# Four engine programs written out for all 16 images in place of a loop, and the offset convolution moved one tile earlier on TensorE

## The chip, the cores and the metric

The kernel runs on one core of one Trainium2 chip. The metric is the device time of one execution in microseconds (us). Of the kernel before there are three such times, with a median of 4523.1 us (4519.83 to 4523.54), and one profiled execution.

## The reference

Sixteen images of 32 channels and 64 x 64 pixels go through four residual steps, each `x = x + f(norm(x))`. The norm subtracts the mean and divides by the standard deviation, for each image and channel.

1. A 3 x 3 convolution written in Winograd form with 6 x 6 tiles: a transform of the input, one product over channels for each of the 36 frequencies, and the inverse transform.
2. A deformable 3 x 3 convolution in 8 groups. A convolution with 18 outputs (the offset convolution) gives for each pixel and tap an offset in y and x; each tap is read by bilinear sampling at the shifted place and then weighted and summed.
3. Four quantised 3 x 3 convolutions one after the other, with weights that are plus or minus a scale, with rounding and clamping between them, and a 1 x 1 branch beside the second.
4. A 3 x 3 convolution plus a product over the absolute vertical differences, and a gate per channel from a small two-layer network on the channel means.

## The kernel before

Everything is in float32, except the three later quantised convolutions, which have bfloat16 operands. The 64 rows of an image are cut into 4 strips; strip and channel together fill 128 partitions, with 1024 pixels each.

The work of three images is interleaved. One period (n) holds 24 slots of 3 tiles, written (slot, tile), as (14, 2). In period n the kernel does the deformable sampling of image n, which is the bulk; step 1, the norm and the offset convolution of image n + 1 (the functions named `a`); steps 3 and 4 of image n - 1 (the functions named `c`); and the first norm of image n + 2 (`first`). The order on each engine is written out by hand in that engine's `slot`.

- TensorE has in each tile a row tile (`row_tile`, L1512, 6 products of 128 x 128 by 128 x 512, from `select` and `image` into `ps_r`), then at tile 0 the folds of the slot before (L1524, L1545), at some tiles the transposes of gathered samples (`turn`, L1538), and then what `a` and `c` have for that tile. `conv_half` (L1498) makes all 3 x 3 convolutions: the offset convolution from `taps_a` (shown as `wino`) into `ps_a`, and those of step 3 from `taps_c` into `ps_c`.
- VectorE multiplies each row tile by column weights (L1217), and works on the gathered samples, the norms and the rounding. It orders its own instructions by a counting semaphore (`Chain`).
- ScalarE makes `select` (L672, L674), copies the image that a period samples into `image` (`place_image`, L683: the first two thirds at the end of the period before, the last third at the head of the period), and takes results out of PSUM.
- SyncE issues transfers in order: the column weights (L481), the 12 shifted copies of the normalised image into `taps_a` (L434, at its slot 12), the store of the activations to a plane in memory (L439, at slots 6, 9 and 12) and the three loads of shifted planes into `taps_c` (L445, at slots 7, 10 and 13). `load_image` (L491, slot 22) brings the next image from the table of patches.
- GpSimd gathers the samples by indirect transfers, 192 for each image, in loops of its own.

`schedule` gives the order of the periods to the other four engines. Periods -2, -1, 0, 15 and 16 are written out; periods 1 to 14 are a hardware loop of 14 turns:

```python
    chain.restart()
    period(0)
    chain.restart()
    with eng.Fori(1, N - 1) as t:
        period(t)
        chain.restart()
    period(N - 1)
```

`restart` waits for the engine's own counting semaphore and clears it. In the loop, waits compare with values computed in registers from the period's number, and some addresses are computed too. The tiles that the change touches on TensorE are (14, 2), which has the third later convolution of step 3 (called conv3 below) and the offset convolution; (5, 2), which has the first convolution of step 3 (conv0) and two frequency products of step 1 (L1451).

Of the kernel before, what the change touches and what calls it, by code (L numbers as in the profile page):

```python
# [12 lines left out]
N, C, H, W = 16, 32, 64, 64  # L13
# [98 lines left out]
def live(n):  # L112
    return not isinstance(n, int) or 0 <= n < N
# [21 lines left out]
class Chain:  # L135
# [8 lines left out]
        return self.n  # L144

    def upto(self, n):
        self.eng.wait_ge(self.sem, n)

    def join(self):
        self.eng.wait_ge(self.sem, self.n)  # L150
# [2 lines left out]
        self.add(ins)  # L153
        self.join()

    def restart(self):
        if self.n:
            self.join()
            self.eng.sem_clear(self.sem)
            self.n = 0  # L160


def schedule(eng, chain, slot, prepare=None):

    def period(n):
        for s in range(SLOTS):
            slot(n, s)

    period(-2)
    period(-1)
    if prepare:
        prepare()
    chain.restart()
    period(0)
    chain.restart()
    with eng.Fori(1, N - 1) as t:
        period(t)
        chain.restart()  # L180
    period(N - 1)
    chain.restart()
    period(N)


def build(nc, x, w0, w1off, w1d, w2t, w2n, wds, w3t, w3e, watt1, watt2, vecs, off_bias, prelu_a, batt1, out):
    with ExitStack() as ctx:
# [175 lines left out]
        def tap_rows(t):  # L363
            return t.rearrange("p (r w) -> p r w", w=XW)
# [214 lines left out]
        @block.gpsimd  # L579
        def _(pool):  # L580
            chain = Chain(pool, pool_chain)
            for t in (values, xn_a, xn_c, act_c):
                nc.gpsimd.memset(t[:], 0.0).then_inc(zeroed, 1)
            pool.wait_ge(zeroed, 4)
            chain.step(nc.gpsimd.memset(same_channel[:], 0.0))
            nc.gpsimd.affine_select(out=ident[:], in_=zeros, compare_op=ALU.not_equal, fill=1.0, base=0,
                                    pattern=[[-1, P]], channel_multiplier=1).then_inc(idents_ready, 1)
            sc = same_channel[:].rearrange("p (s c) -> p s c", c=C)
            for s in range(STRIPS):
                chain.step(nc.gpsimd.affine_select(out=sc, in_=sc, compare_op=ALU.not_equal, fill=1.0 / STRIPS,  # L590
                                                   base=-s * C, pattern=[[0, STRIPS], [-1, C]], channel_multiplier=1))
            nc.gpsimd.memset(eps_col[:], EPS).then_inc(idents_ready, 1)
            pool.wait_ge(idents_ready, 2)

            for half in range(2):
                ps = slice(half * W, half * W + W)
                chain.step(nc.gpsimd.iota(grid_y[ps], pattern=[[2, Q], [1, 3]], base=half - 1,
                                          channel_multiplier=0, allow_small_or_imprecise_dtypes=True))
                chain.step(nc.gpsimd.iota(grid_x[ps], pattern=[[0, 3], [1, 3]], base=-1,
                                          channel_multiplier=1, allow_small_or_imprecise_dtypes=True))  # L600
            chain.step(nc.gpsimd.iota(minus_row[:], pattern=[[0, 1]], base=0, channel_multiplier=-1,
                                      allow_small_or_imprecise_dtypes=True))
            chain.step(nc.gpsimd.memset(one_col[:], 1.0))
            nc.gpsimd.memset(base_row[:], 0.0).then_inc(grid_ready, 1)
            pool.wait_ge(grid_ready, 1)
            chain.restart()
            pool.wait_ge(table_cleared, 16)
            freed = pool.alloc_register("freed")
            pool.reg_mov(freed, 1)
            with pool.Fori(0, N) as n:  # L610
                with pool.Fori(0, PARTS // IDX) as quad:

                    pool.wait_ge(table_out, (n + 1) * TABLE_OUT)
                    for h in range(IDX):
                        pool.wait_ge(idx_placed, n * PARTS + quad * IDX + (h + 1))
                        for j in range(JB):

                            pool.wait_ge(weighted, freed)
                            pool.reg_add(freed, freed, 1)
                            for k in range(GTAPS):  # L620
                                i = j * GTAPS + k
                                nc.gpsimd.indirect_dma_start(  # L622
                                    out=ring[j][:, h % 2, k, :], out_offset=None, in_=table,
                                    in_offset=bass.IndirectOffsetOnAxis(ap=idx_part[:, h, i:i + 1], axis=0),
                                ).then_inc(gathered[(h % 2) * JB + j], 16)
# [245 lines left out]
        def _(dve):  # L871
            v = nc.vector
            chain = Chain(dve, dve_chain)
# [371 lines left out]
            summed = [0]  # L1245

            def gathered_block(n, s, q):


                g, e = divmod(s, DT)  # L1250
                m, h = (n, g + 1) if g < PARTS - 1 else (n + 1, 0)
                if e == 0 and live(n):
                    if q == 0:
                        if s > 0:
                            chain.upto(summed[0])
                        add_columns(n, g, 1)
                        summed[0] = weigh_corners(n, g, 2)
                    if q == 1:
                        chain.upto(summed[0])
                        chain.upto(add_rows(g, 2))  # L1260
                        add_columns(n, g, 2)
                    if q == 2:
                        summed[0] = weigh_corners(n, g, 3)
                if e == 1 and live(n):
                    if q == 0:
                        chain.upto(summed[0])
                        summed[0] = add_rows(g, 3)
                    if q == 1:
                        chain.upto(summed[0])
                        add_columns(n, g, 3)  # L1270
                if e == 2 and live(m):
                    if q == 0:
                        if s == SLOTS - 1:
                            dve.wait_ge(a_dve.sem, a_dve.at(m, "weights"))
                        chain.upto(take_weights(h))
                        summed[0] = weigh_corners(m, h, 0)
                    if q == 1:
                        chain.upto(summed[0])
                        chain.upto(add_rows(h, 0))
                        add_columns(m, h, 0)  # L1280
                    if q == 2:
                        chain.upto(weigh_corners(m, h, 1))
                        summed[0] = add_rows(h, 1)
# [129 lines left out]
        def _(pe):  # L1413
# [28 lines left out]
            def a(n, s, q):  # L1442
                at = (s, q)
# [11 lines left out]
                    mean(a_dve, a_pe, n, "1", mv_a, ps_a)  # L1455
                if at == (11, 1):
                    var(a_dve, a_pe, n, "1", mv_a, ps_a)
                if at == (14, 2):
                    pe.wait_ge(a_dve.sem, a_dve.at(n, "norm1"))
                    pe.wait_ge(taps_a_in, n * COPIES_IN + COPIES_IN)  # L1460
                    for h in range(2):
                        conv_half(ps_a, h, w_off, 0, tap_rows(taps_a)).then_inc(a_pe.sem, 1)
# [66 lines left out]
            def turn(n, g, k):  # L1529
                part = n * PARTS + g  # L1530
                if k == 0:
                    pe.wait_ge(weighted, part * JB + (RING + JB))
                    if not known_zero(n) or g > 0:
                        pe.wait_ge(copied, part * CHUNKS)
                else:
                    pe.wait_ge(copied, part * CHUNKS + k)
                for j in range(JB):
                    ins = nc.tensor.transpose(ps_t[:, j * P:(j + 1) * P],  # L1538
                                              values[:, g % 2, j, chunk_start(k):chunk_start(k) + 4].rearrange("p k c -> p (k c)"), ident[:])
                ins.then_inc(turned, 1)  # L1540
# [62 lines left out]
            def slot(n, s):  # L1603
                g, e = divmod(s, DT)
                for q in range(WT):
                    if live(n):
                        row_tile(n, s, q)
                    if q == 0:
                        fold_before(n, s)
                    if live(n):  # L1610
                        if e == DT - 1 and q != 1:
                            if q == 0 and s in LAST_READ and live(n - 1):
                                pe.wait_ge(c_act.sem, c_act.at(n - 1, LAST_READ[s]))
                            turn(n, g, q // 2)
                    if live(n + 1):
                        a(n + 1, s, q)
                    if live(n - 1):
                        c(n - 1, s, q)
                    if live_s(n + 2):
                        first(n + 2, s, q)  # L1620

# [64 lines left out]
```

## Time and profile before

| | |
|---|---|
| median of three runs | 4523.1 us (4519.83 to 4523.54) |
| the profiled execution | 4541.68 us |
| its span, first to last instruction | 4539.9 us |
| mean granted TensorE clock | 0.970 of full |
| TensorE busy | 4235.0 us, 93% |
| VectorE, ScalarE, GpSimd busy | 65%, 41%, 68% |
| busy share of the DMA engines | mostly 0.7 to 0.8 |

The span is that of one execution under the hardware profiler. Matmuls overlap, so that a busy TensorE isn't one at its peak. Busy shares count an instruction's own time only; time in which an engine waits, branches or issues transfers is idle. "issue" as a releaser means that the engine waited for nothing that the profile shows.

### The profile page before, as it was taken

What the parts mean: (1) busy time and instruction counts of PE and PEld (TensorE: products, weight loads), DVE (VectorE), ACT (ScalarE), POOL (GpSimd) and SP (SyncE); (2) the same over time, 40 slices, a digit from 0 to 9 for tenths busy, and PEclk for the clock granted to TensorE, in tenths of its full rate; (3) what the DMA queues carried; (4) which work ended last, traced back from release to release, by engine and by line L of the source; (5) the groups of instructions that cost most, each with busy time, mean ns of one, the idle gap of its engine ahead of it and who ended that gap; (6) DMA issues with size and microseconds to landing.
All of it is one profiled execution on the core that took longest, in us unless ns stands there. A gap on an engine that the chain in (4) does not pass through costs nothing.

```text
span 4539.9 us, 75043 instructions
## 1 busy us (share of the span) xinstructions
PE 4235.0 (93%) x24997; PEld 2030.2 (45%) x24997; DVE 2948.8 (65%) x6076; ACT 1864.5 (41%) x2023; POOL 3088.7 (68%) x3094
## 2 busy tenths in 40 slices
PE   2899999999999999999999999999999999999993
PEld 2444444444444444444444444444444444444441
DVE  5656676666666766677666666766667666766553
ACT  1434444443434434444344434434444344444431
POOL 1777777676776767667677776767767677676750
PEclk8999999999999999999999999999999999999996
DMA  4687788778877787777778877787777777878862
GB/s 112 214 248 228 235 255 231 230 228 237 238 230 233 223 234 237 219 242 234 227 238 244 243 225 232 225 234 240 223 241 234 225 232 232 245 234 235 244 200 61
DMA packets 480356, 1024.07 MB, mean 226 GB/s; under 512 B 262165, under 2 KB 298357, under 8 KB 475637
## 3 DMA queue, kind: packets, MB, share of 16 engines
q1 hardware_dynamic: 324628, 511.64, 39.0%
q10 hardware_dynamic: 57024, 305.72, 20.0%
q0 software_dynamic: 98304, 201.52, 16.2%
q8 instruction: 233, 3.82, 0.3%
q14 instruction: 167, 1.36, 0.1%
HBM read 862.19 MB, written 73.20 MB: 206 GB/s over the span
## 4 chain that ended last, share of the span: by engine, by line
PE 70%; DMA 11%; SPq 7%; DVE 5%; issue 4%; POOL 2%; ACT 0%; ACTq 0%; DVEq 0%; another core or an unknown queue 0%; POOLq 0%
PE ps_r L1512 50%; PE ps_c L1498 6%; DMA taps_c<-plane_act 5%; PE ps_y L1524 5%; DMA plane_act<-act_c 3%; PE ps_a L1451 3%; SPq L434 3%; PE ps_c L1538 2%; POOL ring L622 2%; DMA wino<-patch_table 1%; PE ps_y L1545 1%; SPq L439 1%; PE ps_a L1489 1%; SPq L491 1%; DVE col_hat L1217 1%
## 5 line engine op out<-in xcount | busy, mean ns | idle before, releaser
L622 POOL DMA_INDIRECT ring<-patch_table,idx_part x3072 | 3080.5, 1003 | 1305.1 <-issue 1168.4
L1512 PE MATMUL ps_r<-select,image 128*128 128x512 f32 x6912 | 3183.7, 607 | 59.9 <-issue 48.3
L1512 PEld LDWEIGHTS ps_r<-select,image 128*128 128x128 f32 x6912 | 1270.3, 192 | 1481.8 <-issue 1459.2
L1217 DVE TENSOR_TENSOR col_hat<-ps_r,col_hat 128x512 f32<-128x512 f32 x1152 | 794.8, 690 | 1366.4 <-PE ps_r L1512 1359.0
L672 ACT ACTIVATE select<-row_in,minus_row 128x1536 f32<-128x1536 f32 x384 | 604.1, 1573 | 778.9 <-PE ps_r L1512 731.5
L674 ACT ACTIVATE select<-select,one_col 128x1536 f32<-128x1536 f32 x384 | 605.3, 1576 | 12.5
L691 ACT COPY samples<-ps_c 128x512 f32<-128x512 f32 x256 | 149.8, 585 | 679.1 <-PE ps_c L1538 679.1
L1524 PEld LDWEIGHTS ps_y<-col_hat,w_dense 128*32 128x32 f32 x9216 | 228.7, 109 | 297.1 <-issue 296.2
L1524 PE MATMUL ps_y<-col_hat,w_dense 128*32 128x128 f32 x9216 | 331.9, 277 | 0.0
L1226 DVE TENSOR_TENSOR ps_w<-ring,ps_w 128x384 f32<-128x384 f32 x512 | 284.7, 556 | 31.1 <-DMA ring<-patch_table,idx_part 21.5
L1232 DVE TENSOR_TENSOR ring<-ring,ps_w 128x384 f32<-128x384 f32 x512 | 280.2, 547 | 4.4
L1228 DVE TENSOR_TENSOR ring<-ring,ps_w 128x384 f32<-128x384 f32 x512 | 280.2, 547 | 0.0
L739 ACT ACTIVATE work_c<-ps_c,bn_bias,bn_scale 128x512 f32<-128x512 f32 x160 | 120.2, 778 | 216.8 <-PE ps_c L1498 202.9
L1242 DVE TENSOR_TENSOR values<-ring 128x192 f32<-128x192 f32 x512 | 182.5, 356 | 19.4
L1498 PE MATMUL ps_c<-taps_c,w_signs 96*32 96x512 bf16 x1152 | 92.7, 462 | 108.3 <-DMA taps_c<-plane_act 77.8
L707 ACT COPY wino<-ps_a 128x384 f32<-128x384 f32 x96 | 46.0, 479 | 310.6 <-PE ps_a L1451 310.6
L1538 PE MATMUL ps_c<-ident,values 128*128 128x128 f32 x1024 | 160.8, 280 | 0.0
L1538 PEld LDWEIGHTS ps_c<-ident,values 128*128 128x128 f32 x1024 | 117.5, 140 | 92.9 <-issue 92.7
L1451 PE MATMUL ps_a<-wino,w_freq 128*128 128x64 f32 x1152 | 141.1, 282 | 16.6 <-DVE wino L998 16.6
L1451 PEld LDWEIGHTS ps_a<-wino,w_freq 128*128 128x128 f32 x1152 | 142.1, 201 | 31.4 <-DVE wino L998 16.7
L1498 PEld LDWEIGHTS ps_c<-taps_c,w_signs 96*32 96x32 bf16 x1152 | 28.4, 107 | 163.6 <-DMA taps_c<-plane_act 90.9
L1498 PE MATMUL ps_a<-wino,w_off 96*32 96x512 f32 x768 | 87.7, 605 | 12.9 <-DMA wino<-xn_a 12.9
(232 smaller groups left out, 2497.3 us busy)
## 6 DMA issues: line engine op xcount, KB each, us to landing
row_in<-coord_table ACTq DMA_DIRECT2D x384, 768.0 KB
col_hat<-coord_table SPq DMA_DIRECT2D x384, 768.0 KB
ring<-patch_table,idx_part POOLq DMA_INDIRECT x3072
taps_c<-plane_act SPq DMA_DIRECT2D x135, 268.1 KB
taps_c<-xn_c SPq DMA_DIRECT2D x186, 130.0 KB
coord_table<-wino SPq DMA_DIRECT2D x64, 216.0 KB
wino<-xn_a SPq DMA_DIRECT2D x93, 130.0 KB
plane_act<-act_c SPq DMA_DIRECT2D x180, 65.0 KB
```

Of the source, the lines that this page charges most:

```text
L622: nc.gpsimd.indirect_dma_start(out=ring[j][:, h % 2, k, :], out_offset=None, in_=table, in_offset=bass.IndirectOffsetOnAxis(ap=idx_part[:, ...
L672: nc.scalar.activation(sel, row_in[s % 2][:], ACT.Abs, bias=minus_row[:]).then_inc(row_in_read, 1)
L674: nc.scalar.activation(sel, sel, ACT.Relu, bias=one_col[:], scale=-1.0).then_inc(select_made, 1)
L1217: v.tensor_tensor(hat_t, ps_r[:, (s + t) % 2], hat_t, ALU.mult).then_inc(tile_weighed, 1)
L1226: chain.add(v.tensor_tensor(lower.rearrange("p k (m c) -> p k m c", c=C), corners[:, :, 2:], by_corner[:, :, 2:], ALU.mult))
L1228: return chain.add(v.tensor_tensor(corners[:, :, 0:2], corners[:, :, 0:2], by_corner[:, :, 0:2], ALU.mult))
L1232: return chain.add(v.tensor_tensor(upper, upper, lower, ALU.add))
L1451: ins = mm(ps_a[:, f % 2, b_ * NT:(b_ + 1) * NT], flat_w(w_freq, f * FREQ + b_), wino_v[:, f, :, b_, :], start=True, stop=True)
L1498: ins = mm(ps[s * C:(s + 1) * C, h], w[:, k0 + dy], src[:, r0:r0 + RS // 2, 0:W], start=(dy == 0), stop=(last and dy == 2))
L1512: ins = mm(ps_r[:, (s + t) % 2], image[:, m, t], select[s % 2][:, m], start=(m == 0), stop=(m == PAIRS - 1))
L1524: ins = mm(ps_y[j * C:(j + 1) * C, :], w_dense[:, DT - 1 - e].rearrange("p g o -> p (g o)"), col_hat[s % 3][:, t, j * P:(j + 1) * P], star ...
L1538: ins = nc.tensor.transpose(ps_t[:, j * P:(j + 1) * P], values[:, g % 2, j, chunk_start(k):chunk_start(k) + 4].rearrange("p k c -> p (k c) ...
```

## The change

`schedule` calls `period` for n from -2 to 16 in a Python loop, so that TensorE, VectorE, ScalarE and SyncE each get a straight program. Waits and addresses become constants. `Chain.restart` goes, and with it the clearing of the semaphore; VectorE's first wait on its chain in a period, which the restart had made needless, is now made. GpSimd keeps its loops.

On TensorE the offset convolution goes from (14, 2) to (14, 1), which is behind that slot's second row tile. In every tile the part `c` now comes ahead of the part `a`. Only (5, 2) has work of both kinds once the offset convolution has moved: conv0 comes ahead of the two frequency products there.

```diff
     def upto(self, n):
-        self.eng.wait_ge(self.sem, n)
+        if n:
+            self.eng.wait_ge(self.sem, n)
...
-    def restart(self):
-        if self.n:
-            self.join()
-            self.eng.sem_clear(self.sem)
-            self.n = 0
-
-
 def schedule(eng, chain, slot, prepare=None):
...
-    def period(n):
+    for n in range(-2, N + 1):
+        if n == 0 and prepare:
+            prepare()
         for s in range(SLOTS):
             slot(n, s)
-
-    period(-2)
-    period(-1)
-    if prepare:
-        prepare()
-    chain.restart()
-    period(0)
-    chain.restart()
-    with eng.Fori(1, N - 1) as t:
-        period(t)
-        chain.restart()
-    period(N - 1)
-    chain.restart()
-    period(N)
...
             pool.wait_ge(grid_ready, 1)
-            chain.restart()
             pool.wait_ge(table_cleared, 16)
...
                     if q == 0:
-                        if s > 0:
-                            chain.upto(summed[0])
+                        chain.upto(summed[0])
                         add_columns(n, g, 1)
...
-                if at == (14, 2):
+                if at == (14, 1):
                     pe.wait_ge(a_dve.sem, a_dve.at(n, "norm1"))
                     pe.wait_ge(taps_a_in, n * COPIES_IN + COPIES_IN)
                     for h in range(2):
...
                             turn(n, g, q // 2)
+                    if live(n - 1):
+                        c(n - 1, s, q)
                     if live(n + 1):
                         a(n + 1, s, q)
-                    if live(n - 1):
-                        c(n - 1, s, q)
                     if live_s(n + 2):
                         first(n + 2, s, q)
```

## Rows read from the trace of the kernel before

**Rows 1.** Waits of TensorE's matmuls: total us, times, longest us.

```profile
PE ps_c L1498 <- DMA taps_c<-plane_act: 77.8, 26, 6.8
PE ps_r L1512 <- issue: 48.3, 13, 6.6
```

**Rows 2.** Timeline of TensorE at a turn's end; start, length, [idle before <-releaser].

```profile
1465.04 4.49 PE L1512 MATMUL ps_r<-select,image 128*128 128x512 f32 x6 [4.02 <-issue]
```

**Rows 3.** The same at the loop's exit, the first row tile of period 15.

```profile
4191.30 2.74 PE L1512 MATMUL ps_r<-select,image 128*128 128x512 f32 x6
```

**Rows 4.** Timeline of TensorE at (14, 2) in four periods of the loop.

```profile
1624.57 5.36 PE L1498 MATMUL ps_a<-wino,w_off 96*32 96x512 f32 x48
1635.12 2.75 PE L1498 MATMUL ps_c<-taps_c,w_signs 96*32 96x512 bf16 x24 [5.20 <-DMA taps_c<-plane_act]
...
1901.01 5.36 PE L1498 MATMUL ps_a<-wino,w_off 96*32 96x512 f32 x48 [0.42 <-DMA wino<-xn_a]
...
2452.62 1.50 PE L1498 MATMUL ps_c<-taps_c,w_signs 96*32 96x512 bf16 x24 [1.00 <-DMA taps_c<-plane_act]
...
4092.51 2.75 PE L1498 MATMUL ps_c<-taps_c,w_signs 96*32 96x512 bf16 x24 [6.46 <-DMA taps_c<-plane_act]
```

**Rows 5.** Windows, two periods: busy (x) of PE, PEld, DVE, ACT, POOL; PEclk; DMA; GB/s.

```profile
2013.90:2285.30 271.40, 264.12 (x1562) 126.11 (x1562) 183.26 (x375) 116.07 (x126) 191.84 (x192) 0.98 0.77 234
2285.30:2553.00 267.70, 261.04 (x1562) 125.36 (x1562) 182.65 (x375) 115.93 (x126) 195.99 (x194) 0.99 0.81 238
```

**Rows 6.** Timeline of GpSimd where the gathers of the next image start.

```profile
1687.84 0.95 POOL L622 DMA_INDIRECT ring<-patch_table,idx_part  x1 [13.92 <-issue]
```

**Rows 7.** Windows behind the end of a turn: columns as in rows 5.

```profile
1465.00:1468.40 3.40, 3.36 (x4) 1.51 (x5) 0.00 (x0) 2.40 (x3) 2.48 (x4) 0.50 0.56 170
1190.30:1195.30 5.00, 4.98 (x6) 1.85 (x6) 0.00 (x0) 4.92 (x4) 3.78 (x5) 0.50 0.65 222
3374.30:3379.90 5.60, 5.60 (x12) 2.03 (x16) 0.10 (x1) 4.07 (x4) 4.28 (x5) 0.50 0.74 232
3100.60:3104.00 3.40, 3.37 (x30) 1.66 (x34) 0.00 (x0) 0.53 (x1) 2.65 (x3) 1.00 0.62 203
```

**Rows 8.** Timeline of ScalarE at the same turn's end as rows 2.

```profile
1459.78 1.67 ACT L683 COPY image<-wino 128x384 f32<-128x384 f32 x2 [2.02 <-DMA wino<-patch_table]
1465.99 1.28 ACT L683 ACT_TABLE_LOAD   x1 [4.06 <-issue]
```

**Rows 9.** Timeline at the turn's end with the latest image: TensorE, then ScalarE.

```profile
2553.03 4.53 PE L1512 MATMUL ps_r<-select,image 128*128 128x512 f32 x6 [3.43 <-issue]
...
2550.30 1.62 ACT L683 COPY image<-wino 128x384 f32<-128x384 f32 x2 [4.15 <-DMA wino<-patch_table]
```

**Rows 10.** Timeline of SyncE's queue in the period of the first lines of rows 4.

```profile
1602.88 8.04 SPq L434 DMA_DIRECT2D wino<-xn_a  x12
1611.03 1.92 SPq L439 DMA_DIRECT2D plane_act<-act_c  x4
1624.13 1.64 SPq L445 DMA_DIRECT2D taps_c<-plane_act  x3
```

**Rows 11.** Windows behind the wait of conv3 in two periods: columns as in rows 5.

```profile
1635.10:1639.10 4.00, 3.98 (x26) 1.56 (x27) 0.00 (x0) 1.95 (x3) 0.27 (x1) 0.50 0.34 122
3270.50:3277.40 6.90, 6.89 (x29) 2.62 (x30) 0.00 (x0) 4.69 (x5) 0.95 (x1) 0.50 0.15 48
```

**Rows 12.** Timeline of TensorE: a short wait at (11, 2), and the row tile behind it.

```profile
1869.83 1.52 PE L1498 MATMUL ps_c<-taps_c,w_signs 96*32 96x512 bf16 x24 [1.99 <-DMA taps_c<-plane_act]
1871.28 4.47 PE L1512 MATMUL ps_r<-select,image 128*128 128x512 f32 x6
```

**Rows 13.** Timeline around (5, 2): TensorE, then ScalarE, then VectorE.

```profile
1527.46 5.36 PE L1498 MATMUL ps_c<-taps_c,w_sign 96*32 96x512 f32 x48
...
1530.32 0.78 ACT L739 ACTIVATE work_c<-ps_c,bn_bias,bn_scale 128x512 f32<-128x512 f32 x1 [2.27 <-PE ps_c L1498]
...
1537.62 0.69 DVE L1293 TENSOR_SCALAR work_c<-work_c 128x1024 f32<-128x1024 f32 x1
```

## The prediction

> **What bounds the kernel.** I read the waits of TensorE first, since the page has it busy for 93% of the span. They name two large groups: 77.8 us for the shifted planes of the later convolutions of step 3, and 48.3 us in 13 waits of the row tile that nothing in the profile ended, "issue" [rows 1]. The timeline then gives their places. The second group is the end of each loop turn: fourteen turns have 13 back edges, and there TensorE stood for 4.0 us, for example, behind the last transposes of the turn [rows 2]. At the exit of the loop the same tile starts with no idle time before it [rows 3], and periods 0 and 15, which are written out, have no such wait. So it belongs to the branch. Of the first group 14 waits lie at conv3, in (14, 2), one in each turn: 64.8 us together, from 1.0 us to the 6.8 us of the waits' longest [rows 1, 4].
>
> The windows over whole periods say what is between the waits. One period had 264.1 us busy in 271.4 us at a mean clock of 0.98, the next 261.0 us in 267.7 us at 0.99 [rows 5]. The missing hundredths are worth 0.02 x 271.4 = 5.4 us and 0.01 x 267.7 = 2.7 us; taken off, both have 258.5 us of work at full clock. A period is this work, plus the waits, plus what the reduced clock costs. No other engine is near it: GpSimd stands for 13.9 us before the gathers of the next image [rows 6], more than the change can take from a period, and VectorE was busy for 183 us in one [rows 5].
>
> **The back edges.** With constants and no branch the 13 waits of 48.3 us go [rows 1]. The clock goes with them. Behind an edge the six matmuls of a row tile took 4.49 us [rows 2] against 2.74 us at the exit [rows 3], and the window there shows half the clock for 3.4 us [rows 7], which is 1.7 us of work lost. Of 13 edges nine are like this, two have 5.0 and 5.6 us at half clock, and two have none (the window at 3100.6 us is one) [rows 7]: 9 x 1.7 + 2.5 + 2.8 = 20.6 us. Gross gain 68.9 us.
>
> What is late next at this place is the image. Its first row tile needs the first image copy of ScalarE, which starts when the transfer from the patch table lands. In the turn of rows 2 TensorE went idle at 1465.04 - 4.02 = 1461.0 us. ScalarE's two copies ran from 1459.78 for 1.67 us [rows 8], so the first ended at about 1460.6, only 0.4 us ahead. At the latest one TensorE went idle at 2553.03 - 3.43 = 2549.6 us, and the first copy ended at 2550.30 + 0.8 = 2551.1 us [rows 9], 1.5 us late. Over the 13 edges this margin lies between 0.8 us early and 1.6 us late; seven are late, by 4.4 us in sum. The second copy has the length of a row tile more. The last third of the image is copied at the head of the period and today waits behind the edge and a table load [rows 8]; at the exit of the loop, with neither, it made no one wait [rows 3]. So I give back between 0 and 6 us, and take 2.5: the 4.4, less a part for the register instructions that SyncE no longer runs between the six image transfers. Net 66.4 us.
>
> The registers in the waits of TensorE cost nothing that I can find: row tile follows row tile at the same distance in periods 0 and 15, with constants, and in the loop. VectorE's added wait is on work of the period before; its end is what the restart waited for anyway. Both at zero, and at most some tenths of a us a period.
>
> **The offset convolution, one tile earlier.** The work of TensorE ahead of conv3 is the same before and after, only in another order. When conv3 can start is set by SyncE's queue: 12 copies of taps for 8.0 us, then the four stores of the plane, then a pause for their landing from 1613 to 1624.1 us, then three loads [rows 10], which landed when TensorE resumed at 1635.1 [rows 4]. No instruction of this chain waits for TensorE's part that moves, so conv3 keeps its time. The moved convolution would start some 3.0 us earlier (a row tile and a set of transposes). Its taps had barely landed: in one period it waited for them by 0.42 us [rows 4], in one by 0.15 us, and in 12 not at all. So in its new place it waits for 0 to 3.4 us in a turn, middle 1.8 us. All of this comes off the wait at conv3, which shrinks from a mean of 64.8 / 14 = 4.6 us to about 2.9. The sum of the waits is unchanged, at zero gain.
>
> What can change is the clock. Twelve of the 14 waits at conv3 are followed by half clock, between 3.7 and 7 us of it [rows 11]; the halves sum to 31 us. A wait in two shorter pieces may bring less of it: after the 1.00 us wait conv3 took 1.50 us and not 2.75 [rows 4], thus full clock, and after one edge of 2.5 us too [rows 7]; but after a wait of 1.99 us at (11, 2) the row tile took 4.47 us [rows 12]. The rows point both ways. Bounds are 0 and 31 us; I take 10, a third, since most waits left at conv3 will still be near 3 us and the edges of that length mostly did cost clock.
>
> The Trainium skill speaks of this too (TensorE: Matmul & The Clock Gate, Why this matters for your kernels): it warns of idle gaps between bursts of matmuls, past a certain length, so that the shorter pieces could keep the clock. This trace agrees only in part, as the rows above show. By that page alone all 31 us would come back.
>
> **conv0 before the frequency products.** conv0 would start 2.8 us earlier in (5, 2). Its taps are in: it didn't wait in any turn, and the smallest distance from landing to start in the loop was 3.2 us. ScalarE now makes two frequency copies behind conv0 and only then its two `affine` steps of 0.78 us [rows 13]; these end some 2.3 us behind TensorE's last product of the tile instead of 0.8. VectorE wants them at 1537.6 us, 4.8 us behind it (1527.46 + 5.36 = 1532.8) [rows 13]. Hidden, zero; if that cover were gone, at most 1.5 us a period.
>
> **Sum.** -48.3 - 20.6 + 2.5 - 10 = -76.4 us, against the profiled execution's 4541.7 us (its span 4539.9): 4465.3. The median of the runs is 18.6 us below the profiled one; with the same saving it becomes 4446.7, and I say 4447 us. Whether the edge costs the same without the profiler is open; a tenth of the saving either way is 8 us.
>
> **The rivals.**
> - The image takes the edge's place. For: its margin is nil [rows 8, 9]. Against: it is late only in seven edges. Were it 1.5 us late everywhere, as in the worst, with 1.7 us of reduced clock, 13 x 3.2 = 42 us come back less the 2.5 already given: 4486 us.
> - The clock behind conv3 recovers wholly, as short waits elsewhere suggest [rows 4]: 21 us more, 4426 us. The rule of the Trainium skill named above (TensorE: Matmul & The Clock Gate) would lead here.
> - The wait moves and does not shrink: what delays the moved convolution delays conv3 too, for example as ScalarE's and VectorE's work of the tile slides behind it. Then 14 x 1.8 = 25 us are added and the 10 not gained: 4482 us.
> - The change doesn't remove the idle time of the edge: "issue" hides another wait of the period's start. Then little but the 10 us changes: 4513 to 4523 us. Against it stands the exit [rows 3].
> - Slower: straight code starves TensorE, because it fetches instructions all the time. A stop would cost as an edge, 3.7 us plus 1.6 of clock. It decides at more than 76.4 / 5.3 = 14 stops, one in each turn; with three in each turn the time is 4447 + 42 x 5.3 = 4670 us. Against it: the loop's body too is far longer than a tile, and periods 0 and 15 ran straight without a stop.
>
> **How the numbers follow.** Forecast 0.67; the image 0.10, the clock 0.12, the wait that stays 0.05, no effect 0.03, slower 0.03. The forecast's own range, from the bounds of image and clock and the tenth for the profiler, is 4430 to 4468. For 8 in 10 it must take in the clock's recovery and part of the way to the image: 4422 to 4482. About 0.2%, or 9 us, is what can be told from no change. Faster by more: 0.94; within: 0.03; slower: 0.03.
>
> **What would show it.** The waits of TensorE lose the row tile's "issue", and at the period's head at most a wait of 1 to 2 us for the image copy stands in its place, with the granted clock at 1.00 there. ScalarE has no table load at the head of the period. A wait for the taps of some 1.8 us appears at the offset convolution, and the one at conv3 is shorter by the same. Periods last 264 to 269 us. It would be wrong if "issue" waits appear within periods, if conv3's wait stays near 4.6 us, or if periods remain above 271 us.

## The result, and the profile after

The changed kernel takes 4404.45 us (median of 4 runs, 4398.95 to 4422.6) against 4523.32 us of the kernel before: a ratio of 0.973, with a 95% interval of 0.968 to 0.978. That is 119 us less. The forecast was 76 us less, 4447 us, with a range down to 4422; the time lies below it. In the profiled executions the span went from 4539.9 to 4401.5 us, 138 us less, since the profiled execution of before was longer than its median.

The waits of TensorE's matmuls in the changed kernel; total us, times, longest us. The first row was too small in the kernel before to be among its large ones; the second answers to the first of [rows 1]:

```profile
PE ps_a L1478 <- DMA wino<-xn_a: 34.2, 15, 11.3
PE ps_c L1478 <- DMA taps_c<-plane_act: 8.0, 11, 1.5
```

The row tile's 48.3 us of "issue" are gone, and so are nearly 70 of the 77.8 us of waits for the shifted planes. The taps of the offset convolution are waited for instead: 22.3 us in 13 of the 14 periods 1 to 14, next to 11.9 us in the two periods ahead of these, which the kernel before has too (12.3 us).

The end of a period, with TensorE and then ScalarE, answers to [rows 2] and [rows 8]:

```profile
1689.14 0.60 PE L1518 MATMUL ps_c<-ident,values 128*128 128x128 f32 x4
1689.58 2.74 PE L1492 MATMUL ps_r<-select,image 128*128 128x512 f32 x6
...
1688.43 1.67 ACT L664 COPY image<-wino 128x384 f32<-128x384 f32 x2 [1.48 <-DMA wino<-patch_table]
```

The row tile follows the transposes at once and takes 2.74 us in place of 4.49. ScalarE's first copy of the image ended at about 1689.3 us, 0.3 us ahead of it.

Slot 14 in the changed kernel answers to [rows 4] and [rows 10]: TensorE, then SyncE's queue, then ScalarE's.

```profile
1582.48 7.05 PE L1478 MATMUL ps_a<-wino,w_off 96*32 96x512 f32 x48 [2.66 <-DMA wino<-xn_a]
1589.47 2.84 PE L1492 MATMUL ps_r<-select,image 128*128 128x512 f32 x6
1592.15 0.60 PE L1518 MATMUL ps_c<-ident,values 128*128 128x128 f32 x4
1592.68 1.59 PE L1478 MATMUL ps_c<-taps_c,w_signs 96*32 96x512 bf16 x24
...
1569.68 1.99 SPq L421 DMA_DIRECT2D plane_act<-act_c  x4
...
1583.20 1.23 SPq L427 DMA_DIRECT2D taps_c<-plane_act  x3
...
1592.79 0.52 ACTq L643 DMA_DIRECT2D row_in<-coord_table  x1
```

The wait ahead of the offset convolution is there, and the conv3 behind the transposes doesn't wait. From the first plane load to conv3's start are 1592.68 - 1583.20 = 9.5 us, in which the load has landed; before, in [rows 4, 10], 1635.12 - 1624.13 = 11.0 us passed until it had landed. The last line is the one that my steps lacked. In the kernel before the same load of ScalarE's queue, and the copy that stands ahead of it in ScalarE's program, were here:

```profile
1624.68 0.59 ACT L691 COPY samples<-ps_c 128x512 f32<-128x512 f32 x1 [5.00 <-PE ps_c L1538]
1624.83 0.55 ACTq L662 DMA_DIRECT2D row_in<-coord_table  x1
```

It brings 768 KB for a later `select`. It was issued 0.7 us behind the first plane load; now it is issued 9.6 us behind it. Over periods 1 to 14 it was issued from 1.1 us ahead of the first plane load to 2.0 us behind it before, and 7.6 to 9.6 us behind it after. The queues between issue and landing of the plane loads, first before (1624.2 to 1635 us), then after (1583.2 to 1589.9 us), show it. q1 is SyncE's, q10 ScalarE's, q0 GpSimd's; the columns are packets, MB and the share of 16 engines:

```profile
q1 hardware_dynamic: 258, 1.48, 52.4%
q10 hardware_dynamic: 143, 0.79, 29.3%
q0 software_dynamic: 209, 0.43, 15.4%
...
q1 hardware_dynamic: 234, 1.35, 75.9%
q0 software_dynamic: 97, 0.18, 13.1%
```

In the first stretch ScalarE's queue moved 0.79 MB, which is that load; in the second nothing. Over periods 2 to 14 the plane loads of conv3 took 10.4 us on average from first issue to last landing before, and 7.3 us after.

Two whole periods of the changed kernel, with the columns of [rows 5]:

```profile
1425.40:1689.60 264.20, 261.11 (x1565) 125.32 (x1564) 182.76 (x376) 113.52 (x125) 190.93 (x192) 0.99 0.80 241
1689.60:1951.40 261.80, 259.42 (x1564) 125.04 (x1563) 182.47 (x376) 114.47 (x126) 193.37 (x193) 1.00 0.80 243
```

A period takes 260.5 to 265.4 us (period 1, 272.4), where I had said 264 to 269. The second one ran at full clock throughout and was busy for 259.4 us, which is close to the 258.5 us of work that [rows 5] gave.

### The profile page after: what moved, and what is told of

Same layout as the page of the kernel before. It is cut to its first block, busy times and chain, and to the rows that moved or that the text cites. A ratio compares the mean times of both kernels' runs of the same rounds, so it can differ in the third digit from the quotient of the medians.

```text
span 4401.5 us, 67257 instructions
## 1 busy us (share of the span) xinstructions
PE 4188.2 (95%) x24997; PEld 2019.2 (46%) x24997; DVE 2947.0 (67%) x6076; ACT 1833.4 (42%) x2008; POOL 3076.9 (70%) x3094
## 4 chain that ended last, share of the span: by engine, by line
PE 76%; DMA 8%; SPq 5%; DVE 5%; POOL 3%; issue 2%; ACTq 0%; ACT 0%; POOLq 0%; DVEq 0%
PE ps_r L1492 54%; PE ps_c L1478 6%; PE ps_y L1504 5%; DMA wino<-xn_a 4%; PE ps_a L1431 3%; POOL ring L603 3%; SPq L416 3%; DMA taps_c<-plane_act 3%; PE ps_c L1518 2%; PE ps_a L1478 2%; PE ps_y L1525 1%; PE ps_a L1469 1%; DMA taps_c<-xn_c 1%; PE ps_c L1573 1%; PE ps_c L1551 1%
## 5 line engine op out<-in xcount | busy, mean ns | idle before, releaser
L1492 PE MATMUL ps_r<-select,image 128*128 128x512 f32 x6912 | 3147.4, 601 | 11.7 <-DVE col_hat L1198 7.2
L655 ACT ACTIVATE select<-select,one_col 128x1536 f32<-128x1536 f32 x384 | 605.4, 1577 | 12.5
L1478 PE MATMUL ps_c<-taps_c,w_signs 96*32 96x512 bf16 x1152 | 78.6, 400 | 38.9 <-DMA taps_c<-act_c 30.8
L1478 PE MATMUL ps_c<-taps_c,w_edge_conv 96*32 96x512 f32 x768 | 89.0, 613 | 14.4 <-DMA taps_c<-xn_c 14.4
## 6 DMA issues: line engine op xcount, KB each, us to landing
taps_c<-plane_act SPq DMA_DIRECT2D x135, 268.1 KB
```

The costliest lines, as they stand in the source:

```text
L655: nc.scalar.activation(sel, sel, ACT.Relu, bias=one_col[:], scale=-1.0).then_inc(select_made, 1)
L1478: ins = mm(ps[s * C:(s + 1) * C, h], w[:, k0 + dy], src[:, r0:r0 + RS // 2, 0:W], start=(dy == 0), stop=(last and dy == 2))
L1492: ins = mm(ps_r[:, (s + t) % 2], image[:, m, t], select[s % 2][:, m], start=(m == 0), stop=(m == PAIRS - 1))
```

## The experiments

The theory after the result (A): ScalarE's `row_in` load stands in its program behind its copy of the second transposes of slot 14. With the offset convolution ahead of those transposes, the load goes out about 8 us later and no longer shares the DMA engines with the plane loads of conv3. The rival (B): the straight programs by themselves, without register instructions and restarts, took conv3's wait away.

### The TensorE order alone, in the loop

```diff
-                if at == (14, 2):
+                if at == (14, 1):
...
+                    if live(n - 1):
+                        c(n - 1, s, q)
                     if live(n + 1):
                         a(n + 1, s, q)
-                    if live(n - 1):
-                        c(n - 1, s, q)
```

> Only the TensorE order of the change: the offset convolution in (14, 1) and part c ahead of part a; the loop of 14 turns stays. Theory A: ScalarE's next row_in load stands in its program behind the copy of the second transposes of slot 14. With the convolution ahead of those transposes the load is issued some 8 us later and no longer competes with the three plane loads, which land in about 7.3 us in place of 10.4. So the wait at conv3 (4.9 us a turn) nearly goes, some 1.6 us of wait appears at the offset convolution, and with the half clock that goes too the time is about 4455 us. Theory B: the conv3 wait went because the programs are straight (no register instructions, no restart). Then conv3 still waits for about 3 us here, and the time is 4510 to 4520 us.

Measured: 4488.7 us, ratio 0.992 (0.989 to 0.995), or 36 us less. Waits of TensorE:

```profile
PE ps_r L1512 <- issue: 42.2, 12, 5.5
PE ps_a L1498 <- DMA wino<-xn_a: 41.5, 16, 11.3
PE ps_c L1498 <- DMA taps_c<-plane_act: 14.3, 16, 3.3
```

The mechanism is A's: the planes' waits fall from 77.8 to 14.3 us while the loop stays, and the plane loads take 7.7 us. The size is not. I had said 4455; the taps cost 29 us of new waits in periods 1 to 14 and not 22, and in two turns TensorE waited for the image at the head, 4.6 us in all.

### The writing out alone

The changed kernel with the two edits of the experiment before taken back.

> Only the writing out: four engines straight, the offset convolution in (14, 2), part a ahead of part c. Theory A: the plane loads take 10 to 11 us as before, conv3 waits for 4 to 5 us in each period; only the 13 edges with their clock go: about 4455 us, and conv3's wait is the largest of TensorE. Theory B: the conv3 wait is gone here too, and the time is within 10 us of the changed kernel's, 4395 to 4415 us.

Measured: 4448.8 us, ratio 0.984 (0.981 to 0.987), 76 us less on the median.

```profile
PE ps_c L1478 <- DMA taps_c<-plane_act: 58.5, 15, 6.6
```

No "issue" wait of the row tile remains. Over periods 2 to 14 conv3 waits for 3.7 us on average, against 4.9 before, and its plane loads take 9.6 us. My sum had priced this part at 66.4. B is out as the main cause. The two halves give 76 + 36 = 112 of the 119 us.

### The load early again in the changed kernel

`rows_ahead` issues the `row_in` load, as a rule at the head of ScalarE's slot; here that of slot 15 goes out in slot 14, ahead of the copy of the second transposes.

```diff
-                if s != SLOTS - 2:
+                if s not in (15, SLOTS - 2):
                     rows_ahead(n, s)
...
+                if s == 14:
+                    rows_ahead(n, 15)
                 if e == DT - 1 and live(n):
                     turn(n, g, 1)
```

> The changed kernel, in which ScalarE issues the row_in load that stands at the head of its slot 15 in slot 14, ahead of its copy of the second transposes. Theory A: the load runs beside the plane loads again; these take 10 to 10.5 us in place of 7.3, conv3 waits for 2 to 3 us in each period, part of it with half clock behind: 4435 to 4455 us. Rival: the place of this load doesn't matter, and the time stays within 5 us of the changed kernel's 4404 us.

Measured: 4448.8 us, ratio 0.984 (0.981 to 0.987). One load at another place in ScalarE's program costs 44 us against the changed kernel, and 36 us by the spans of the two profiled executions. ScalarE's queue, TensorE and SyncE's queue in slot 14:

```profile
1585.20 0.52 ACTq L643 DMA_DIRECT2D row_in<-coord_table  x1
...
1600.44 1.50 PE L1480 MATMUL ps_c<-taps_c,w_signs 96*32 96x512 bf16 x24 [2.59 <-DMA taps_c<-plane_act]
...
1590.23 1.23 SPq L427 DMA_DIRECT2D taps_c<-plane_act  x3
```

The load goes out 5.0 us ahead of the plane loads, somewhat earlier than in the kernel before, and these land 1600.44 - 1590.23 = 10.2 us after their issue. The waits for planes are 32.6 us in 17, of which 29.9 us lie at conv3.

### The load late, the convolution not moved

To the writing out alone, this is added. `a_early` holds ScalarE's two steps on the result of the offset convolution:

```diff
-                if s != SLOTS - 2:
+                if s not in (15, SLOTS - 2):
                     rows_ahead(n, s)
                 if live(n + 1):
                     a_early(n + 1, s)
+                if s == 15:
+                    rows_ahead(n, s)
```

> The straight kernel with the offset convolution in (14, 2) (part a first), in which ScalarE issues the row_in load of its slot 15 behind its two steps on the offset convolution's result. Theory A: without the move, the later load alone brings the plane loads to about 7.3 us and conv3's wait from 4.9 to 1.8 us, and the taps are not waited for: 4410 to 4425 us. Rival: the move itself is needed, the load's place is a side effect: 4450 to 4460 us, as with the writing out alone.

Measured: 4408.0 us, ratio 0.974 (0.971 to 0.977), 41 us less than the writing out alone, and the time of the changed kernel within the measurement.

```profile
1588.44 0.52 ACTq L643 DMA_DIRECT2D row_in<-coord_table  x1
...
1583.01 5.36 PE L1480 MATMUL ps_a<-wino,w_off 96*32 96x512 f32 x48
1589.34 1.50 PE L1480 MATMUL ps_c<-taps_c,w_signs 96*32 96x512 bf16 x24 [0.97 <-DMA taps_c<-plane_act]
...
1582.13 1.24 SPq L427 DMA_DIRECT2D taps_c<-plane_act  x3
```

The plane loads land after 1589.34 - 1582.13 = 7.2 us. The offset convolution is in its old place and doesn't wait. Conv3 waits for 21.6 us in sum, where the changed kernel waits for 1.6 us there and 22.3 us at the taps. So what the move gains can be had from the place of this load alone, within the measurement.

The other traces bear this out. In each of those in which the load goes out 4.9 us or more behind the first plane load, the plane loads take 7.2 to 7.7 us on average. In those in which it goes out within 2.5 us of it, they take 8.3 to 10.4 us.

### The offset convolution ahead of the second transposes

The changed kernel with the offset convolution in (14, 2), between the row tile and the transposes.

```diff
                     if live(n):
                         row_tile(n, s, q)
...
+                    if live(n + 1) and (s, q) == (14, 2):
+                        pe.wait_ge(a_dve.sem, a_dve.at(n + 1, "norm1"))
+                        pe.wait_ge(taps_a_in, (n + 1) * COPIES_IN + COPIES_IN)
+                        for h in range(2):
+                            conv_half(ps_a, h, w_off, 0, tap_rows(taps_a)).then_inc(a_pe.sem, 1)
                     if live(n):
                         if e == DT - 1 and q != 1:
```

> The changed kernel with the offset convolution back in (14, 2), but ahead of that tile's second transposes. Theory A (the row_in load waits behind those transposes): the load stays late, the plane loads take about 7.3 us and conv3 doesn't wait; and the convolution starts 2.6 us later, so that the 1.6 us of wait for its taps go: 14 x 1.6 = 22 us less than the changed kernel, 4380 to 4392 us. Rival: the taps land later with it, or the wait comes back at conv3: 4400 to 4410 us.

Measured: 4393.7 us, ratio 0.971 (0.966 to 0.976). That is 11 us below the changed kernel, with intervals that overlap. Both ran again side by side, five times each.

> The changed kernel once more, beside the next three on the same chip: 4395 to 4415 us.

> The changed kernel with the offset convolution in (14, 2) ahead of the second transposes, once more beside it. If the wait for the taps (22 us over the periods) went for less than it gave back at conv3 (16 us), it is 10 to 20 us faster than the changed kernel; if the two cancel, within 5 us.

Measured: 4395.5 us for the changed kernel (0.9725, 0.9705 to 0.9744), 4404.6 us for this one (0.974, 0.972 to 0.976). No gain. The waits of TensorE, of the changed kernel in that run and then of this one:

```profile
PE ps_a L1478 <- DMA wino<-xn_a: 29.3, 15, 11.3
PE ps_c L1478 <- DMA taps_c<-plane_act: 4.2, 7, 0.8
...
PE ps_c L1473 <- DMA taps_c<-plane_act: 26.4, 19, 3.7
PE ps_a L1473 <- DMA wino<-xn_a: 11.4, 1, 11.4
```

The 18 us of waits for the taps are gone and 22 us have come at the planes, 15.6 of them at conv3 of periods 1 to 14. Conv3's start is set by the landing of its planes there: most of what isn't waited for ahead of it is waited for at it.

### Two periods in a turn

```diff
-    with eng.Fori(1, N - 1) as t:
+    with eng.Fori(1, N - 1, 2) as t:
         period(t)
         chain.restart()
+        period(t + 1)
+        chain.restart()
```

> The kernel before, with two periods in each turn of the loop: 7 turns, 6 back edges in place of 13; the restarts stay at each period. If the stop belongs to the taken branch: 7 x (3.7 + 1.6) = 37 us less than before, 4485 us, and 6 waits of the row tile in place of 13. If it belongs to the restart of the chains or to the start of a period: 13 waits, and the time of before.

Measured: 4490.4 us, ratio 0.9925 (0.989 to 0.996), 34 us less by the ratio.

```profile
PE ps_r L1514 <- issue: 22.1, 6, 4.0
```

Six waits in place of 13, of 3.7 us on average. The restarts are still made in every period, so the stop doesn't belong to them but to the taken branch.

### TensorE alone straight

Of the four engines only TensorE has both no chain semaphore and a `prepare`, so the condition takes it alone.

```diff
+    if chain.sem is None and prepare:
+        for n in range(-2, N + 1):
+            if n == 0:
+                prepare()
+            period(n)
+        return
```

> The kernel before, with TensorE's program alone written out; VectorE, ScalarE and SyncE keep their loops and stops. Theory: the others' stops of 3 to 4 us are hidden behind TensorE's work: nearly all of the 69 us go, 4455 to 4465 us, as with all four. Rival: TensorE then waits at the head of the period for ScalarE's last image third (edge plus table load) or for VectorE's tile: a wait of 1 to 3 us stays at each edge, 4480 to 4500 us.

Measured: 4448.6 us, ratio 0.983 (0.978 to 0.987), the time of the writing out of all four, and below the 4455 to 4465 us that I had said.

```profile
PE ps_r L1519 <- issue: 0.9, 2, 0.6
PE ps_r L1519 <- ACT image L690: 5.9, 10, 1.1
```

The stops of ScalarE's, VectorE's and SyncE's loops are covered, up to 8.8 us: these image waits and 2.9 us for `select`. The plane loads of conv3 took 8.3 us here and not the 9.6 of the writing out alone, with the `row_in` load as near to them; why is left open.

### A hint ahead of the branch

The kernel before, in which each of the four engines names at the head of a turn the place of the branch to come.

```diff
-    with eng.Fori(1, N - 1) as t:
+    with eng.bass.Fori(1, N - 1, hint_back_edge=True, engines=bass.OrderedEngineSet([eng.engine])) as t:
```

> The kernel before, loop and all, with a hint at the head of each turn on each of the four engines that names the place of the branch to come. If the stop is the fetch of the loop's first instructions, most of the 48 us of waits and of the clock behind them go: 4455 to 4475 us. If it is the branch and the registers themselves: the time of before, 4515 to 4525 us.

Measured: 4468.1 us, ratio 0.986 (0.981 to 0.991), 62 us less by the ratio. The loop, its registers and restarts are all there:

```profile
PE ps_r L1512 <- issue: 4.4, 2, 3.3
PE ps_r L1512 <- ACT image L683: 3.1, 5, 1.7
```

The 48.3 us are down to 4.4. Since branch, registers and restarts are still there and only the branch's place is told ahead, the stop was the fetch of the instructions behind the branch. The Trainium skill says that a taken branch out of the fetched pages forces a fetch of the target before execution goes on (Runtime: NRT & Kernel Launch, Instruction fetch mechanics); this case agrees, with 3.7 us on average for each of the 13 edges without the hint.

### The swap of parts undone

The changed kernel with `a` ahead of `c` again, the offset convolution staying in (14, 1).

> The changed kernel with part a ahead of part c in every tile again, the offset convolution staying in (14, 1). In (5, 2) two frequency products come ahead of conv0 again. My step said that this edit is hidden: the time within 5 us of the changed kernel's. Rival: the swap bears part of the gain, since conv0 starts 2.8 us earlier: 10 to 20 us slower.

Measured: 4396.5 us, ratio 0.972 (0.969 to 0.974), against 4395.5 of the changed kernel beside it. The swap does nothing that can be measured.

### The column load behind the planes held back

```diff
+                if s == 14 and live(n) and live(n + 1):
+                    sp.wait_ge(a_pe.sem, a_pe.at(n + 1, "offconva"))
                 if live(n + ahead // SLOTS) and s != SLOTS - 2:
```

> The kernel of e5 with one more wait on SyncE: the col_hat load that it issues right behind the three plane loads in slot 14 is held until the first half of the offset convolution is done. If the plane loads are slowed by any 768 KB load beside them, they take 5 to 6 us in place of 7.3, conv3's wait of 1.1 us goes, and the time is 10 to 16 us below e5's, some 4375 us. If the queue serves them in order, they stay at 7.3 us and the time stays; if the load comes too late for slot 16, VectorE makes TensorE wait there and it is slower.

Measured: 4392.0 us, ratio 0.972 (0.969 to 0.9745); the intervals of this one and of the kernel it is built on overlap. On the medians it is 12.5 us below that kernel, and I had said 10 to 16 us if any load beside the planes slows them. But the plane loads took 7.5 us in both, where I had said 5 to 6 us, and the waits at conv3 are 22.3 us against 17.1, so that the lower time can't be put down to them. The load was held for 2 us only, for example from 1.3 to 3.4 us behind the first plane load, so this is a weak test. It shows no slowing by a load that stands behind the planes in the same queue, where ScalarE's load in another queue, as soon behind them, cost 3 us.

## Why the prediction was wrong

**What bounds the kernel** held. The work of a period was given as 258.5 us, and a period at full clock was busy for 259.4.

**The back edges** held, in size too. All 13 stops went with their clock; writing out alone gave 76 us where the sum of this part was 66.4. Some 10 us of waits at conv3 went with it, which I hadn't priced: 54.5 us in place of 64.8. The 2.5 us given back to the image were 0.3 us in the changed kernel. That the stop belongs to the branch was argued from [rows 3]; the two-period loop has shown it, and the hint that it is the fetch.

**conv0 ahead of the products** cost nothing that can be measured, as said; the swap was tried. VectorE's added wait was not tried by itself. It is in the writing out alone, whose gain was not below its sum.

**The offset convolution** is where it failed. The step reads: "No instruction of this chain waits for TensorE's part that moves, so conv3 keeps its time." The first half is right for SyncE's queue, the only one I followed. But the chain contains transfers, and their length depends on what else the DMA engines do. Moving 5.4 us of TensorE's work ahead of the second transposes delays these transposes; ScalarE's copy waits for them, and behind that copy its `row_in` load is queued. The prediction names neither this copy nor the load behind it. The load had gone out within 2.0 us of the first plane load; it now goes out 7.6 to 9.6 us behind it, and the plane loads landed in 7.3 us in place of 10.4. Of 64.8 us of waits at conv3 1.6 were left, while the offset convolution's waits rose from 0.6 to 22.3 us: 41.5 us less, where I had put zero. The load early again cost 44 us, and the load late without the move gained 41.

**The clock behind conv3** was taken as a third of 31 us. With hardly a wait left at conv3, half clock was seen in three places of the periods 1 to 14, 3.4 us each, besides one near the start of period 1 that the kernel before has too. The three are all at waits for the taps of 2.0 us or more. So some 26 us came back in the profiled executions. One of the rivals had this term, with 31 us, but from shorter waits; here the waits weren't cut in pieces, they went. The "all 31 us" of that rule doesn't follow either: with 1.8 us off, the longest wait at conv3 would have stayed at 5.0 us in one piece, and behind each of the 11 stops of 3.3 us or more at the edges half clock was seen. The taps' waits of 2.26 and 2.36 us left the clock alone, while those of 2.04, 2.66 and 3.25 us did not, so the length alone doesn't decide, as [rows 7, 12] had it. Two of them, the second with full clock:

```profile
3422.10 7.05 PE L1478 MATMUL ps_a<-wino,w_off 96*32 96x512 f32 x48 [2.04 <-DMA wino<-xn_a]
...
2370.37 5.36 PE L1478 MATMUL ps_a<-wino,w_off 96*32 96x512 f32 x48 [2.36 <-DMA wino<-xn_a]
```

**The range** had a slip too. By its own bounds, with no wait for the image, all of the clock and a tenth more, the low end is 4447 - 2.5 - 21 - 8 = 4415.5 us and not 4430. The measured time lies below this as well, so the slip isn't why the range missed.

The sum by what was measured in the profiled executions: 48.1 us of edges, 20.6 of their clock, 41.5 of conv3 and taps, 26 of clock behind conv3, some 4 us of waits and 5 of clock at (11, 2), less 3 of new waits for the taps of step 4's convolution: 142 us, against 138 by which the spans differ. TensorE's idle time fell by 91.6 us, which fits the 91 us of waits in this sum, and its busy time by 46.8 us, from 4235.0 to 4188.2; so the 52 us of clock are some 5 too many. My sum was 76, 62 us short in the profiled executions: the 41.5 us at conv3 and taps that I had at zero are the largest part, the clock behind conv3, 26 us for 10, the next. The medians differ by 119 us.

## What to carry to other kernels

When a piece of work moves on one engine, follow what waits for its neighbours on every other engine, and there read on past the instruction that is released to the transfers queued behind it. A transfer is not a fixed length: ask which large transfer of another queue will now run beside it, and which will no longer. Where a hardware loop's body is long and the engine that bounds the kernel takes the branch, its stop can be read from the trace at the first instruction of each turn, and a hint or the writing out of that one engine's program takes most of it: 62 and 78 us here by the ratios, where writing out all four engines' gave 73.

## What the runs showed of the hardware

- A taken back edge stopped TensorE for 2.5 to 6.6 us, 3.7 on average, and cost 1.7 to 2.8 us more in 11 of 13 cases by half the clock behind it. With a branch hint two stops were left in 13, of 3.3 and 1.1 us.
- Three plane loads of 268.1 KB took 7.3 us beside no other queue's large load, and 10.4 us when a 768 KB load of ScalarE's queue was issued within 2 us of them. With TensorE's program alone straight they took 8.3 us beside that load, and this is not explained. The Trainium skill says that the DMAs issued from the engines' queues run on the same 16 DMA engines and interleave (Trainium Kernel Development and Optimization, Key Constraints); this case agrees, with 3 us for it.
- At the head of each turn ScalarE loaded its activation table for 1.28 us [rows 8]; in straight code these loads weren't there (33 table loads in the execution in place of 48). With TensorE's program alone straight all 48 are there, and the time is that of the writing out of all four, so they cost nothing that can be measured.
